# A graph network on one core: VectorE's loop over the turns of the spline passes written out with constants

## The chip, the core and the metric

The kernel runs on one core of a Trainium2 chip. The core's engines run their own instruction streams beside each other: TensorE (PE in the profile, its weight loads PEld) multiplies matrices into PSUM, VectorE (DVE) and ScalarE (ACT) work on tiles in SBUF and PSUM, GpSimd (POOL) issues here the indirect DMAs that gather rows, SyncE (SP) issues plain DMAs. They keep order among themselves by counting semaphores: one engine raises a count, another waits until it has reached a value. The metric is the time of one execution on the device in microseconds (us); lower is better.

## What is computed

A graph with 12500 nodes of 32 features and 212500 edges (source, destination, sorted by destination) goes through four parts, each closed by a residual and a layer norm: two GIN convolutions, two steps of normalised GCN propagation, three spline convolutions with batch norm, and an attention layer with four heads. The change lies in the spline convolutions. Cut to what matters:

```python
def _basis(edge_attr):
    v = edge_attr * (KS - 1)
    lo = jnp.floor(v)
    f = v - lo
    ...
    w = jnp.where(bits[None] == 1, f[:, None, :], 1.0 - f[:, None, :])
    basis = jnp.prod(w, axis=-1)
    wi = idx[..., 0] + KS * idx[..., 1] + KS * KS * idx[..., 2]
    return (basis, wi)

def _sconv(x, src, dst, basis, wi, W, R, b):
    n = x.shape[0]
    z = jnp.einsum('nc,kco->nko', x, W)
    msg = jnp.zeros((src.shape[0], W.shape[2]), x.dtype)
    for s in range(basis.shape[1]):
        msg = msg + basis[:, s, None] * z[src, wi[:, s]]
    agg = jax.ops.segment_sum(msg, dst, num_segments=n)
    cnt = jax.ops.segment_sum(jnp.ones((dst.shape[0],), x.dtype), dst, num_segments=n)
    agg = agg / jnp.clip(cnt, 1.0)[:, None]
    return agg + x @ R + b
```

## The kernel before, in words

**Passes.** The edges are handled in 1664 tiles of 128. The kernel makes a pass over them for each aggregation: gin1, gin2, gcn1, gcn2, sp1, sp2, sp3, and a last one ("collect" and "apply") for attention. In each, GpSimd gathers 128 source rows for a tile by one indirect DMA (L779), 1664 times in a spline pass (fewer in the first four, where part of the edges is handled through counts). Between two passes a node phase turns the sums into new features, and SyncE stores these as the table from which the next pass gathers.

**A spline pass.** 16 tiles are a half (104 in a pass, `HALVES`), four halves a turn (26, `TURNS`). The gathered rows go into a ring of four halves (`RING`), with one semaphore for each quarter of a slot. For half k GpSimd waits until VectorE has used the rows of half k - 4 (`u_ready`), then issues 16 gathers; it has no loop here, and its indices are in SBUF. TensorE loops over pairs of halves. VectorE runs `moments`: a prologue, then a loop of 25 turns (L1925), then the last turn written out (L1927). Both call `turn_(i, last)`.

**VectorE's turn.** For each of its four halves it makes the next half's one-hots (L1834), loads 16 places from SBUF into registers (L1894), waits for a cleared moment buffer, and then goes through 16 tiles. For each tile it adds TensorE's product to the moments at a place that a register names (`add_moments`, L1878); each addition waits for the one before it (`mom_added`) and, for each pair of tiles, for TensorE (`mom_ps`). For each pair it also makes the next right-hand sides (`one_hot_basis`, L1866), for each four tiles the next weighted rows (`weight_rows`, L1631), which wait for the gather's quarter; the next half's basis is made in four steps (L1845 to L1854), and once a half the aggregate is added (`add_aggregate`, L1886). TensorE may be up to eight tiles ahead of the additions.

**Waits.** Every `wait_ge` with a value that depends on the loop's index i gets this value from an operation of the engine's sequencer on a register (`Signal.done(phase, k)` is k plus a constant, and k is 64, 16 or 4 times i and so on). Most go through `hold` (L531), some are written in place (L1875, L1884). Where i is a Python number, the value is a constant in the instruction. TensorE's, ScalarE's and GpSimd's streams are built by functions of their own.

Of the kernel before, what the change touches and what calls it, by code (L numbers as in the profile page):

```python
# [47 lines left out]
TURNS = ET // (RING * G)  # L48
# [81 lines left out]
def build(nc, x, src_tile, dst_tile, dst_base, half_base, src_row, dst_ext, attr_tile, gW1, gb1, gW2, gb2, gW3, gb3,  # L130
          gW4, gb4, sW, sR, sb_, sg, sbe, aw, fc_w, fc_b, abias, out):
    ctx = ExitStack()
    with ctx:
# [1286 lines left out]
        def _(dve):  # L1420
# [410 lines left out]
            def moments(p):  # L1831
# [29 lines left out]
                def one_hot_basis(k, h, t):  # L1861
                    if t == 0:
                        hold(dve, "dve", close_made, k + (1 + halves * SPLINE.index(p)))
                        dve.wait_ge(basis_made.sem, basis_made.done(p, k))
                    hold(dve, "dve", mom_ps.sem, mom_ps.done(p, G * k + t + 1 - AHEAD))
                    v.tensor_tensor(vb[:, t % AHEAD:t % AHEAD + 2, :, :],  # L1866
                                    bs[:, h, t:t + 2, KS:].unsqueeze(3).broadcast_to([P, 2, K12, TW]),
                                    oh_close[:, h, t:t + 2, :].unsqueeze(2).broadcast_to([P, 2, K12, TW]),
                                    ALU.mult).then_inc(v_ready.sem, 2)
# [10 lines left out]
                def add_aggregate(k, h):  # L1880

                    first = dve.value_load(half_prev[0:1, bass.ds(k, 1)], min_val=0, max_val=N)
                    hold(dve, "dve", agg_ps.sem, agg_ps.done(p, k))
                    dve.wait_ge(agg_added.sem, agg_added.done(p, k - 1))  # L1884
                    to = acc[0:C, bass.ds(first, GW)]
                    v.tensor_tensor(to, to, ps[0:C, 4 + h, 0:GW], ALU.add).then_inc(agg_added.sem, 1)  # L1886
# [35 lines left out]
                weight_rows(p, 0, 0, 0, 1, close=True, uses=1)  # L1922
                for t in range(0, AHEAD, 2):
                    one_hot_basis(0, 0, t)
                with dve.Fori(0, TURNS - 1) as i:  # L1925
                    turn_(i, False)
                turn_(TURNS - 1, True)  # L1927
                add_aggregate(HALVES, 0)

            def places_in_half():  # L1930
# [369 lines left out]
```

## Time and profile before

| what | value |
|---|---|
| median of three plain runs | 14349.69 us (14349.25 to 14349.75) |
| profiled execution, span | 19275.3 us |
| TensorE, weight loads | 49%, 32% of the span |
| VectorE | 37% |
| ScalarE | 10% |
| GpSimd | 53% |
| mean granted TensorE clock | 0.697 of full speed |

The profile is of one execution with the hardware profiler on; on one core nothing lies around its span, which is therefore also the profiled execution's own time. It is 4926 us longer than the median of the plain runs. A row of the trace tells how an operation went in the profiled execution, and how long it took there. "Idle before" is the time that the engine had nothing running before an operation, and the name after the arrow is what the trace believes to have ended it: "issue" when nothing that it shows was waited for, "remote" when the setter of the semaphore isn't known. DVEq is VectorE's sequencer, whose register, semaphore and branch instructions are not counted as busy. A half of a spline pass begins at each L1834.

### The profile page before, as it was taken

What the parts mean: (1) busy time and instruction counts of PE and PEld (TensorE: products, weight loads), DVE (VectorE), ACT (ScalarE), POOL (GpSimd) and SP (SyncE); (2) the same over time, 40 slices, a digit from 0 to 9 for tenths busy, and PEclk for the clock granted to TensorE, in tenths of its full rate; (3) what the DMA queues carried; (4) which work ended last, traced back from release to release, by engine and by line L of the source; (5) the groups of instructions that cost most, each with busy time, mean ns of one, the idle gap of its engine ahead of it and who ended that gap; (6) DMA issues with size and microseconds to landing.
All of it is one profiled execution on the core that took longest, in us unless ns stands there. A gap on an engine that the chain in (4) does not pass through costs nothing. (4 is left out here: it accounts for less than half of the span.)

```text
span 19275.3 us, 188067 instructions
## 1 busy us (share of the span) xinstructions
PE 9537.3 (49%) x45542; PEld 6085.6 (32%) x45542; DVE 7105.4 (37%) x21441; ACT 1838.2 (10%) x1460; POOL 10279.3 (53%) x10674
## 2 busy tenths in 40 slices
PE   4444567774555554555554555554555554002224
PEld 2222222223333333433333333333344333002224
DVE  3333311112212213444444444444444444024446
ACT  3333400000000000000000000000000000000000
POOL 4555545545555554555554555554555554775551
PEclk6666667787766776777776777766777776556657
DMA  4545534444555552000000000000000001111111
GB/s 140 174 164 172 187 95 133 134 133 133 192 183 170 187 188 78 10 10 10 10 10 11 10 10 10 10 10 11 10 10 10 10 10 20 30 33 42 40 38 39
DMA packets 1034937, 1386.17 MB, mean 72 GB/s; under 512 B 318866, under 2 KB 477748, under 8 KB 1033909
## 3 DMA queue, kind: packets, MB, share of 16 engines
q10 hardware_dynamic: 550576, 1115.62, 16.5%
q0 software_dynamic: 338944, 197.81, 6.5%
q1 hardware_dynamic: 144518, 64.56, 1.5%
q14 instruction: 799, 6.55, 0.1%
q8 instruction: 100, 1.64, 0.0%
HBM read 1075.22 MB, written 302.01 MB: 71 GB/s over the span
## 5 line engine op out<-in xcount | busy, mean ns | idle before, releaser
L779 POOL DMA_INDIRECT work<-tab_sp,nodes x4992 | 4721.1, 946 | 4065.7 <-DVE work L1631 2242.7
L981 PE MATMUL ps<-work 128*128 128x192 f32 x9984 | 2766.1, 421 | 3662.8 <-DVE work L1631 2861.9
L981 PEld LDWEIGHTS ps<-work 128*128 128x128 f32 x9984 | 2051.2, 239 | 4251.7 <-DVE work L1878 2592.1
L1878 DVE TENSOR_TENSOR work<-work,ps 128x192 f32 x4992 | 1751.9, 351 | 3741.2 <-remote 1784.2
L779 POOL DMA_INDIRECT work<-tab_att,nodes x1664 | 1691.5, 1017 | 1096.2 <-issue 713.6
L779 POOL DMA_INDIRECT work<-tab_gcn,nodes x1664 | 1585.4, 953 | 1257.0 <-PE ps L875 693.6
L902 PE MATMUL ps<-nodes,work 128*96 128x384 bf16 (+1 forms) x6664 | 1976.1, 418 | 529.4 <-issue 328.8
L1709 DVE TENSOR_TENSOR big<-big,ps 32x12 f32 (+2 forms) x3936 | 619.3, 157 | 3809.0 <-remote 1487.8
L966 PE MATMUL ps<-work,wk 128*32 128x144 f32 x10080 | 1983.3, 355 | 69.2 <-issue 66.9
L779 POOL DMA_INDIRECT work<-in_x,idx x1248 | 1234.9, 990 | 1151.6 <-PE ps L875 738.0
L966 PEld LDWEIGHTS ps<-work,wk 128*32 128x32 f32 x10080 | 1250.9, 135 | 771.3 <-issue 510.7
L1298 ACT ACTIVATE work<-zero 128x2496 f32<-128x2496 f32 x318 | 725.4, 2282 | 7597.5 <-PE ps L966 3660.7
L875 PE MATMUL ps<-work 128*32 128x12 f32 (+2 forms) x7872 | 564.0, 199 | 1708.0 <-DVE big L1709 963.7
L1866 DVE TENSOR_TENSOR work<-work,ps 128x384 f32<-128x384 f32 x2496 | 1366.3, 548 | 32.6 <-issue 29.4
L779 POOL DMA_INDIRECT work<-tab_h,idx x1024 | 984.5, 961 | 737.4 <-PE ps L875 368.5
L902 PEld LDWEIGHTS ps<-nodes,work 128*96 128x96 bf16 (+1 forms) x6664 | 902.2, 142 | 1316.5 <-issue 859.2
L1003 PE MATMUL ps<-work 128*128 128x144 f32 x3584 | 557.0, 319 | 1240.5 <-issue 912.4
L875 PEld LDWEIGHTS ps<-work 128*32 128x32 f32 (+2 forms) x7872 | 479.2, 136 | 2040.6 <-DVE big L1709 1130.5
L887 PE MATMUL ps<-nodes 128*128 128x396 bf16 x2496 | 722.8, 428 | 745.4 <-ACT nodes L1256 354.4
L1256 ACT ACTIVATE nodes<-ps 128x1188 bf16<-128x1188 f32 x832 | 932.9, 1160 | 1394.9 <-remote 729.0
L1003 PEld LDWEIGHTS ps<-work 128*128 128x128 f32 x3584 | 516.7, 214 | 1281.7 <-issue 946.6
L1780 DVE TENSOR_TENSOR big<-big,ps 96x12 f32 (+2 forms) x2720 | 450.0, 165 | 1208.4 <-issue 775.2
(234 smaller groups left out, 6244.2 us busy)
## 6 DMA issues: line engine op xcount, KB each, us to landing
nodes<-counts_d ACTq DMA_DIRECT2D x468, 1056.0 KB
counts_d<-nodes ACTq DMA_DIRECT2D x104, 2376.0 KB
nodes<-counts_d ACTq DMA_DIRECT2D x144, 1320.0 KB
work<-counts_d ACTq DMA_DIRECT2D x117, 1056.0 KB
work<-tab_sp,nodes POOLq DMA_INDIRECT x4992
work<-edge_rows SPq DMA_DIRECT2D x112, 320.0 KB
edge_rows<-work ACTq DMA_DIRECT2D x104, 320.0 KB
work<-tab_gcn,nodes POOLq DMA_INDIRECT x1664
```

Source lines behind the costliest of these rows:

```text
L779: pool.indirect_dma_start(out=rows(p, r)[:, t, 0:ROW[p]], out_offset=None, in_=TABLE[p], in_offset=bass.IndirectOffsetOnAxis(ap=place, axi ...
L875: last = nc.tensor.matmul(ps[0:m, bank, q * LW:(q + 1) * LW], row(q), oh_near(p)[:, h, s * SUB + q, :], start=True, stop=True)
L887: last = nc.tensor.matmul(ps[:, 3 * (b % 2) + q, 0:w], lo_oh[:, (b // SUB) % 2, b % SUB, :], code_oh[:, b % 4, q * w:(q + 1) * w], start=T ...
L902: last = nc.tensor.matmul(to, part[:, t, 0:m], got, start=(t == 0 and m == sides[0][1]), stop=(t == NT - 1 and m == sides[0][1]))
L966: last = nc.tensor.matmul(ps[0:C, 4 + h, 0:GW], wk[:, l, kk, :], mom[:, 1 - h, kk, 0:GW], start=(kk == 0), stop=(kk == K12 - 1))
L981: last = nc.tensor.matmul(moment_place(t), u0[:, s % 2, t % SUB, :], vb[:, t % AHEAD, :, :].rearrange("p k j -> p (k j)"), start=True, sto ...
L1003: last = nc.tensor.matmul(ps[:, 4 + h, 0:GW], weighed[:, s, t % SUB, :], near_half[:, h, t, :], start=(t == 0), stop=(t == G - 1))
L1256: nc.scalar.activation(out_[:, :, :, b, :], ps[:, 3 * (b % 2):3 * (b % 2) + 3, 0:CODES // 3] .rearrange("p q (m w) -> p q m w", w=LW), ACT ...
L1298: return nc.scalar.activation(mom[:, h, :, :], zero[:, :].unsqueeze(2).broadcast_to([P, K12, GW + TW]), ACT.Copy)
L1709: v.tensor_tensor(window, window, ps[0:m, sums_bank(p, s), q * LW:(q + 1) * LW], ALU.add)\
L1866: v.tensor_tensor(vb[:, t % AHEAD:t % AHEAD + 2, :, :], bs[:, h, t:t + 2, KS:].unsqueeze(3).broadcast_to([P, 2, K12, TW]), oh_close[:, h, ...
L1878: v.tensor_tensor(to, to, got, ALU.add).then_inc(mom_added.sem, 1)
```

## The change

VectorE's loop over the first 25 turns and the separate last turn become one Python loop of 26 turns. Each turn's instructions then stand in the program once for each turn, with Python numbers in place of the register i: the values of waits, the offsets into `loc`, `all_attr`, `offs` and `half_prev`. The places that are loaded into registers are still loaded. The order of VectorE's operations and what they wait for stay as they are, and no other engine's stream is edited.

```diff
@@ -1922,9 +1922,8 @@
                 weight_rows(p, 0, 0, 0, 1, close=True, uses=1)
                 for t in range(0, AHEAD, 2):
                     one_hot_basis(0, 0, t)
-                with dve.Fori(0, TURNS - 1) as i:
-                    turn_(i, False)
-                turn_(TURNS - 1, True)
+                for i in range(TURNS):
+                    turn_(i, i == TURNS - 1)
                 add_aggregate(HALVES, 0)
 
             def places_in_half():
```

## Rows read from the trace of the kernel before

**Rows 1.** The page's head and its busy times by engine.

```profile
span 19275.3 us, 188067 instructions
PE 9537.3 (49%) x45542; PEld 6085.6 (32%) x45542; DVE 7105.4 (37%) x21441; ACT 1838.2 (10%) x1460; POOL 10279.3 (53%) x10674
```

**Rows 2.** Stretches (from:to, us): gin1, sp1, sp2, sp3; length; PE, PEld, DVE, ACT, POOL.

```profile
32.00:2389.00 2357.00, 1136.63 (x6220) 565.13 (x6217) 820.23 (x3321) 917.39 (x821) 1233.97 (x1247) 0.67 0.50 167
...
7460.00:10248.00 2788.00, 1504.92 (x6503) 1080.25 (x6504) 1299.46 (x3552) 238.02 (x116) 1572.85 (x1664) 0.73 0.07 10
10359.00:13228.00 2869.00, 1495.52 (x6500) 1078.47 (x6500) 1296.70 (x3546) 238.02 (x116) 1572.27 (x1664) 0.72 0.07 10
13339.00:16120.00 2781.00, 1514.56 (x6502) 1086.78 (x6503) 1301.91 (x3551) 238.02 (x116) 1572.52 (x1663) 0.73 0.07 10
```

**Rows 3.** The same view, sum of the eight stretches between passes and at the end.

```profile
sum 1337.30, PE 767.06 PEld 536.38 DVE 783.57 ACT 125.42 POOL 67.79; mean PE 95.88 PEld 67.05 DVE 97.95 ACT 15.68 POOL 8.47
```

**Rows 4.** Line 779: durations (ns, minimum/median/maximum), then what GpSimd waited for (us, times).

```profile
L779 POOL DMA_INDIRECT work<-tab_sp,nodes x4992: 938/944/1133, 7459.5 to 16120.2; - x200
L779 POOL DMA_INDIRECT work<-tab_gcn,nodes x1664: 938/944/4298, 4436.3 to 7333.3; - x185
L779 POOL DMA_INDIRECT work<-tab_att,nodes x1664: 938/944/2403, 16290.8 to 18907.9; - x185
L779 POOL DMA_INDIRECT work<-in_x,idx x1248: 938/944/2787, 32.2 to 2389.1; - x179
L779 POOL DMA_INDIRECT work<-tab_h,idx x1024: 938/944/9179, 2568.4 to 4268.3; - x171
...
  issue: 3396.7, 10064
  DVE work L1631: 2242.7, 291
```

**Rows 5.** Timeline of GpSimd in sp1: start, length, operation, [idle before].

```profile
9014.61 0.95 POOL L779 DMA_INDIRECT work<-tab_sp,nodes  x1 [0.31 <-issue]
9015.86 0.95 POOL L779 DMA_INDIRECT work<-tab_sp,nodes  x1 [0.30 <-issue]
```

**Rows 6.** Timeline of VectorE in sp1, then the page's group for L1878.

```profile
9014.85 0.35 DVE L1878 TENSOR_TENSOR work<-work,ps 128x192 f32 x1 [3.88 <-remote]
...
L1878 DVE TENSOR_TENSOR work<-work,ps 128x192 f32 x4992 | 1751.9, 351 | 3741.2 <-remote 1784.2
```

**Rows 7.** Timeline of VectorE: half 0 of sp2 (looped), then half 101 of sp1.

```profile
10466.94 0.36 DVE L1834 TENSOR_TENSOR ps<-iota_f,loc 128x192 f32<-128x192 f32 x1
...
10480.98 0.36 DVE L1834 TENSOR_TENSOR ps<-iota_f,loc 128x192 f32<-128x192 f32 x1
...
10262.62 0.35 DVE L1834 TENSOR_TENSOR ps<-iota_f,loc 128x192 f32<-128x192 f32 x1
...
10277.02 0.35 DVE L1834 TENSOR_TENSOR ps<-iota_f,loc 128x192 f32<-128x192 f32 x1
```

**Rows 8.** Line 1925 on VectorE's sequencer; then line 1834's idle before it (us, times).

```profile
L1925 DVEq COMPARE_BRANCH  x75: 55/63/63, 7661.3 to 16108.3; - x75
...
  issue: 178.4, 72
```

**Rows 9.** Timeline of VectorE at one of the loop's branches.

```profile
8956.78 0.68 DVE L1631 TENSOR_TENSOR work<-work,ps 128x512 f32<-128x512 f32 x1
8959.70 0.37 DVE L1834 TENSOR_TENSOR ps<-iota_f,loc 128x192 f32<-128x192 f32 x1 [2.24 <-issue]
```

**Rows 10.** Lines 1875 and 531 on VectorE's sequencer, durations in ns.

```profile
L1875 DVEq ALU_OP  x2475: 2/40/1398, 7567.9 to 16107.6; - x191
...
L531 DVEq ALU_OP  x4926: 1/40/1396, 29.0 to 19188.9; - x198
```

**Rows 11.** Instruction queue (packets, MB) in a looped turn (8957:9063), then 10235.3:10311.

```profile
q14 instruction: 6, 0.05, 0.2%
...
q14 instruction: 3, 0.02, 0.1%
```

## The prediction

> **What bounds the kernel now.** I read the page's first part, then the table of stretches, then GpSimd's gathers, and only then VectorE around the edited loop. The page says that no engine is full: GpSimd 53%, TensorE 49%, VectorE 37% [rows 1]. It also says that the profiled execution takes 19275 us, where the median of the plain runs is 14350 us. So 4926 us of what the trace shows is not in the time that I have to predict, and the first question is which waits those are.
>
> The stretches show where the profiled time lies: the first gin pass 2357 us, the three spline passes 2788, 2869 and 2781 us [rows 2]; the eight stretches between passes and at the end together 1337 us [rows 3]. In every pass GpSimd issues gathers of 128 rows, 10592 in all (4992 + 1664 + 1664 + 1248 + 1024) [rows 4]. Undisturbed, they start 1.25 us apart, 0.95 us of it busy [rows 5]. 10592 x 1.25 = 13240 us. That leaves 14350 - 13240 = 1110 us for what lies between passes, where the profile has 1337 us. The two fit with little left over: the plain run can be explained as gathers back to back in all passes, plus the stretches between. If the stretches between took all of their 1337 us in the plain run too, the spacing would be (14350 - 1337) / 10592 = 1.23 us. I take the gathers as the bound.
>
> In the profiled execution it looks different: GpSimd waits 2243 us for VectorE's L1631 (a slot of the ring that is not yet used up) [rows 4], so there VectorE's chain is the late one, at 2788 / 104 = 26.8 us for a half of 16 tiles. But look at what VectorE itself waits for: L1878 sits 3.9 us for a "remote" release, and 1784 us in all for that reason, a semaphore whose setter the trace doesn't show [rows 6]. Where these waits are absent, the same work is far quicker. A half of the second spline pass, still in the loop, takes 14.04 us from one L1834 to the next (10466.94 to 10480.98); a half of the last turn, which is already written out with constants, 14.40 us (10262.62 to 10277.02) [rows 7]. A half's gathers need 16 x 1.25 = 20.0 us. So without the waits VectorE and TensorE have 5 to 6 us of slack in each half, and GpSimd may run up to four halves ahead.
>
> **The change part by part.** It touches VectorE alone; no DMA, no other queue, no operation on data moves.
>
> The branch. The loop's COMPARE_BRANCH runs 75 times [rows 8]. After it VectorE starts nothing for 2.24 us in the example (from the end of L1631 to L1834) [rows 9]; over the three passes 72 such idles add up to 178.4 us, 2.5 us each [rows 8]. Written out, they go. For a half that is 2.5 / 4 = 0.6 us, which makes the loop's half 14.0 + 0.6 = 14.7 us against 20.0 us of gathers. Hidden: 0 us on the path. Were the cover gone, it is 178 us. The cover is the gathers' pace together with the ring.
>
> The Trainium skill ("Runtime: NRT & Kernel Launch", section on instruction fetch mechanics) says that a taken branch to code outside a small window stops the sequencer for a fetch, and that unrolling is preferred for this. The trace agrees on the idle after the branch. By that page one would book the whole idle as gain; by the gathers' spacing none. What it does here, if VectorE is the bound, is the first rival.
>
> The counted values. Each wait against a counter of the loop costs an ALU_OP of 40 ns on VectorE's sequencer: 2475 of them at L1875, and part of the 4926 at L531 (that line serves all passes) [rows 10]. Upper bound, as if all lay on the path and all of L531 belonged here: (2475 + 4926) x 0.040 = 296 us. Lower bound: the written-out half is 0.36 us longer than the looped one [rows 7], so nothing, or 75 x 4 x 0.36 = 108 us of loss. These operations run while the engine still works on the instruction before, and the addresses that come from loaded registers stay. I take 0, as the two halves are the nearest rows.
>
> The code. VectorE's turn stands 25 times more in each spline pass. One looped turn already fetches 6 instruction packets of 8 KB, most of the last turn 3 [rows 11], and no idle of the branch's kind shows in that last turn. So the fetches are not new; 0 us, hidden as above, with the branch's 2.5 us as the price of any fetch that isn't ready.
>
> The start and the end of a pass. After the last gather VectorE works off what remains, in the last turn, which was constant before. It stays as it is: 0 us.
>
> Sum: 14350 + 0 (branch, hidden) + 0 (values) + 0 (code) = 14350 us; in the profile's own time, the same edits act on a late VectorE, so 19275 should fall by 178 us and up to some 450 us although the median doesn't. The two times part company here, and the median is what is predicted.
>
> **The rivals.** First, VectorE's chain is the bound of the spline passes in the plain run too. For that the gathers must be faster than the trace shows: if the 0.30 us between two gathers is the profiler's, the spacing is 0.95 us and a half's gathers take 15.2 us; and part of VectorE's waits must be real. Then 178 us come back: 14350 - 178 = 14172 us, at the extreme 14172 - 296 = 13876 us. For it speaks that GpSimd really waits on L1631 in the profile. Against it: 10592 x 0.95 = 10062 us, plus 1337 us, leaves 2951 us that real waits must fill in just the amount that makes up the total, where the spacing of 1.25 us closes the sum without any.
>
> Second, it is the bound in some stretches alone, such as the first turns of a pass, and a third of the stalls counts: 14350 - 60 = 14290 us.
>
> Third, slower: straight code needs a new packet again and again, and if a fetch is late at two places of each turn where there was one branch, that is another 2.5 us x 75 = 187 us on VectorE: 14537 us. It decides only once a half of VectorE's work passes 20.0 us; with 14.7 + 0.6 = 15.3 us it doesn't, and it would need the first rival's conditions besides. Against it also stands the last turn without such idles.
>
> Fourth, that the edit does nothing because the values are still computed at run time: the last turn, built by the same function, has constants already, so this is put with "no change".
>
> **How the numbers follow.** Hidden behind the gathers: 0.76, within 14335 to 14365 us. VectorE bound: 0.12. Partly bound: 0.08. Slower by fetches: 0.04. The likeliest gives 14350 us. About 0.2% (29 us) is what a measurement of this kernel can tell from no change. The range reaches down to 14170 us, which takes in the partial case and half of the first rival, and up to 14370 us; what is left out is the other half of that rival, 0.04 of the slower one and a little of the likeliest. Faster by over 0.2%: 0.12 + 0.08 = 0.20; within 0.2%: 0.76; slower: 0.04.
>
> **What would show it.** In the changed profile: L1834's 178 us of idle gone (branch step); no ALU_OP at L1875 (values); no new idles marked "issue" spread over a turn (code); gathers 1.25 us apart as now; and GpSimd's wait for L1631 smaller. A median unchanged beside a shorter profiled span would confirm that the profiled waits aren't the plain run's. A median 100 us or more lower says that the spacing of 1.25 us is the profiler's own and that the first step, the bound, was read wrongly.

## The result: 22 us slower, 1.0016 of the time before

Over 20 runs each, the kernel after takes 14373.93 us (median; 14364.24 to 14382.41), the kernel before 14351.69 us (14343.21 to 14360.93). The ratio is 1.0016, 95% interval 1.001 to 1.0022. That is within the 0.2% that the prediction took as the limit of what can be told, but 20 runs do tell it from zero. The predicted 14350 us is 24 us off, and the range (14170 to 14370) ends 4 us below the median.

The first surprise is in the profile of after: its span is the plain run's time. Head, busy times, instruction queue and the chain that ended last:

```profile
span 14370.1 us, 179464 instructions
PE 8641.1 (60%) x45542; PEld 5702.3 (40%) x45542; DVE 7136.0 (50%) x21441; ACT 1825.6 (13%) x1460; POOL 10256.8 (71%) x10674
...
q14 instruction: 592, 4.85, 0.1%
...
POOL 65%; issue 22%; PE 4%; DVE 3%; DMA 3%; ACT 1%; DVEq 1%; ACTq 0%; SPq 0%; POOLq 0%
```

The edit does what it says: 8603 instructions fewer than in [rows 1], the same 21441 operations on data on VectorE, and 592 instruction packets in the whole run. And GpSimd is the bound: its gathers are 65% of the chain, "issue" (mostly the 0.30 us before each gather) another 22%.

For the comparison, the first profile of the kernel before (19275 us) is no use. The experiment before_again profiled it anew, on a chip where it took the 14351 us of the plain runs. Its head and the same parts:

```profile
span 14350.2 us, 188067 instructions
PE 8595.6 (60%) x45542; PEld 5663.4 (39%) x45542; DVE 7128.7 (50%) x21441; ACT 1827.0 (13%) x1460; POOL 10241.1 (71%) x10674
...
q14 instruction: 799, 6.55, 0.1%
```

The two spans are 19.9 us apart, close to the 22.2 us of the medians, so this pair of traces holds what is to be explained. It lies in the three spline passes. Table of stretches, from the first gather of a pass to its last (from:to, length; PE, PEld, DVE, ACT, POOL; granted clock), before_again, then after:

```profile
5506.40:7593.00 2086.60, 1410.63 (x6697) 1039.65 (x6698) 1350.12 (x3660) 244.88 (x119) 1578.86 (x1664) 0.80 0.09 14
7652.50:9733.90 2081.40, 1407.64 (x6698) 1033.23 (x6699) 1348.11 (x3659) 244.37 (x119) 1574.53 (x1664) 0.81 0.09 14
9793.30:11873.80 2080.50, 1409.34 (x6696) 1036.03 (x6696) 1349.06 (x3657) 244.87 (x119) 1573.59 (x1664) 0.80 0.09 14
sum 6248.50, PE 4227.61 PEld 3108.92 DVE 4047.28 ACT 734.12 POOL 4726.98; mean PE 1409.20 PEld 1036.31 DVE 1349.09 ACT 244.71 POOL 1575.66
```

```profile
5508.40:7599.80 2091.40, 1433.37 (x6698) 1054.95 (x6699) 1349.78 (x3660) 244.89 (x119) 1583.66 (x1664) 0.80 0.09 13
7659.50:9746.60 2087.10, 1415.83 (x6698) 1041.32 (x6699) 1352.87 (x3659) 244.56 (x119) 1580.17 (x1664) 0.81 0.09 13
9806.30:11894.80 2088.50, 1429.94 (x6697) 1053.22 (x6698) 1352.85 (x3659) 244.90 (x119) 1581.62 (x1664) 0.80 0.09 13
sum 6267.00, PE 4279.14 PEld 3149.49 DVE 4055.50 ACT 734.35 POOL 4745.45; mean PE 1426.38 PEld 1049.83 DVE 1351.83 ACT 244.78 POOL 1581.82
```

The sums differ by 18.5 us, and the last column of busy times, GpSimd's own, differs by 4745.45 - 4726.98 = 18.5 us. So the loss is not a wait: the same 4992 gathers take longer. The group of L779 says it once more, with what GpSimd waited for (before_again, then after):

```profile
L779 POOL DMA_INDIRECT work<-tab_sp,nodes x4992 | 4729.6, 947 | 1725.3 <-issue 1519.4 <-DMA tab_sp<-xc 204.1 <-DVE work L1631 1.8
```

```profile
L779 POOL DMA_INDIRECT work<-tab_sp,nodes x4992 | 4748.0, 951 | 1726.0 <-issue 1520.7 <-DMA tab_sp<-xc 204.7 <-DVE work L1631 0.6
```

A mean of 951 ns instead of 947 is 18.4 us in all. The wait for VectorE (L1631), 2243 us in [rows 4], is 1.8 and 0.6 us here. I count extra time from 0.943 us (the median is 0.944) and call a gather long from 0.953 us on: in after 374 of the 4992 are long, by 38.1 us together, against 159 by 19.4 us in before_again. In both, 2.5 us of it is one gather of 3.4 us near the start of sp1.

Which are the long ones? Timeline of GpSimd and VectorE in after (start, length, operation, [idle before]; TensorE's lines left out):

```profile
8094.05 0.55 DVE L1866 TENSOR_TENSOR work<-work,ps 128x384 f32<-128x384 f32 x1
8094.51 0.35 DVE L1845 SCALAR_TENSOR_TENSOR hat<-nodes,iota_f 128x192 f32<-128x192 f32 x1
8094.60 1.09 POOL L779 DMA_INDIRECT work<-tab_sp,nodes  x1 [0.30 <-issue]
...
8095.99 0.95 POOL L779 DMA_INDIRECT work<-tab_sp,nodes  x1 [0.30 <-issue]
...
8097.07 0.69 DVE L1631 TENSOR_TENSOR work<-work,ps 128x512 f32<-128x512 f32 x1 [0.38 <-DMA work<-tab_sp,nodes]
...
8097.24 0.95 POOL L779 DMA_INDIRECT work<-tab_sp,nodes  x1 [0.30 <-issue]
...
8098.40 0.25 DVE L1851 TENSOR_SCALAR hat<-hat 128x192 f32<-128x192 f32 x1
8098.49 0.98 POOL L779 DMA_INDIRECT work<-tab_sp,nodes  x1 [0.30 <-issue]
```

The gather at 8094.60 starts 0.09 us into L1845 and takes 1.09 us; the one at 8098.49 starts 0.09 us into the shorter L1851 and takes 0.98 us. The one at 8097.24, in the middle of L1631, takes 0.95 us. I assigned every gather of the spline passes to the VectorE operation in which it starts:

| VectorE operation at the gather's start | what it reads and writes | after: gathers, long, extra us | before_again |
|---|---|---|---|
| L1845 | nodes, iota_f (SBUF) to hat (SBUF) | 239, 194, 25.3 | 45, 31, 3.15 |
| L1849 | hat twice, to hat (SBUF) | 5, 3, 0.42 | 71, 55, 4.9 |
| L1851 | hat to hat (SBUF) | 242, 151, 7.89 | 21, 7, 0.43 |
| L1854 | hat twice, to work (SBUF) | 9, 9, 1.45 | 55, 48, 7.36 |
| L1834 | iota_f, loc (SBUF) to PSUM | 6, 2, 0.21 | 20, 8, 0.9 |
| L1866, L1878, L1631 | one operand in SBUF, one in PSUM | 3164, 5, 0.06 | 3144, 3, 0.05 |
| other operations | | 37, 5, 2.68 | 53, 4, 2.6 |
| none | | 1290, 5, 0.09 | 1583, 3, 0.05 |

(The expectations count by the operation that runs 46 ns after the gather's start; that moves some gathers that aren't long from row to row, so they have 512 and 196 gathers in the four basis steps, where this table has 495 and 192. The long ones are the same.)

The theory from this (collisions): a gather's start is held up while VectorE runs an instruction that reads two operands in SBUF, or one that reads SBUF alone and writes SBUF. The rival: the written-out code itself costs the time, and the long gathers are chance.

### The profile page after: what moved, and what is told of

It reads as the page before. It is cut to its first block, busy times and chain, and to the rows that moved or that the text cites. A ratio compares the mean times of both kernels' runs of the same rounds, so it can differ in the third digit from the quotient of the medians.

```text
span 14370.1 us, 179464 instructions
## 1 busy us (share of the span) xinstructions
PE 8641.1 (60%) x45542; PEld 5702.3 (40%) x45542; DVE 7136.0 (50%) x21441; ACT 1825.6 (13%) x1460; POOL 10256.8 (71%) x10674
## 4 chain that ended last, share of the span: by engine, by line
POOL 65%; issue 22%; PE 4%; DVE 3%; DMA 3%; ACT 1%; DVEq 1%; ACTq 0%; SPq 0%; POOLq 0%
POOL work L779 65%; DMA work<-tab_gcn,nodes 2%; PE ps L902 1%; DMA work<-in_x,idx 1%; PE ps L887 1%; PE ps L875 1%; PE ps L1086 0%; ACT nodes L1256 0%; PE ps L1003 0%; DVEq L1699 0%; PE ps L1097 0%; PE ps L1062 0%; PE ps L1114 0%; ACTq L1376 0%; DVE big L1780 0%
## 5 line engine op out<-in xcount | busy, mean ns | idle before, releaser
L779 POOL DMA_INDIRECT work<-tab_sp,nodes x4992 | 4748.0, 951 | 1726.0 <-issue 1520.7
L981 PE MATMUL ps<-work 128*128 128x192 f32 x9984 | 2660.2, 410 | 1949.0 <-DVE work L1631 1903.4
L981 PEld LDWEIGHTS ps<-work 128*128 128x128 f32 x9984 | 1983.7, 231 | 2526.3 <-issue 2233.7
L779 POOL DMA_INDIRECT work<-tab_att,nodes x1664 | 1602.7, 963 | 627.0 <-issue 627.0
L1878 DVE TENSOR_TENSOR work<-work,ps 128x192 f32 x4992 | 1740.9, 349 | 567.3 <-DVE work L1878 204.4
L779 POOL DMA_INDIRECT work<-tab_gcn,nodes x1664 | 1589.0, 955 | 553.5 <-issue 492.4
L902 PE MATMUL ps<-nodes,work 128*96 128x384 bf16 (+1 forms) x6664 | 1741.7, 383 | 165.8 <-DMA nodes<-counts_d 103.5
L966 PE MATMUL ps<-work,wk 128*32 128x144 f32 x10080 | 1752.3, 326 | 2.3 <-DVE work L1878 2.3
L1631 DVE TENSOR_TENSOR work<-work,ps 128x512 f32<-128x512 f32 x1248 | 856.8, 687 | 1537.5 <-DMA work<-tab_sp,nodes 1533.6
L779 POOL DMA_INDIRECT work<-in_x,idx x1248 | 1271.3, 1019 | 408.7 <-issue 373.7
L1866 DVE TENSOR_TENSOR work<-work,ps 128x384 f32<-128x384 f32 x2496 | 1364.4, 547 | 0.0
L966 PEld LDWEIGHTS ps<-work,wk 128*32 128x32 f32 x10080 | 1144.4, 124 | 550.5 <-issue 359.7
L779 POOL DMA_INDIRECT work<-tab_h,idx x1024 | 983.8, 961 | 332.3 <-issue 332.0
L875 PE MATMUL ps<-work 128*32 128x12 f32 (+2 forms) x7872 | 507.5, 197 | 1177.0 <-DMA work<-tab_gcn,nodes 707.0
L902 PEld LDWEIGHTS ps<-nodes,work 128*96 128x96 bf16 (+1 forms) x6664 | 836.3, 132 | 784.1 <-issue 394.8
L887 PE MATMUL ps<-nodes 128*128 128x396 bf16 x2496 | 666.0, 406 | 270.6 <-ACT nodes L1256 195.6
```

The source lines that it names most:

```text
L779: pool.indirect_dma_start(out=rows(p, r)[:, t, 0:ROW[p]], out_offset=None, in_=TABLE[p], in_offset=bass.IndirectOffsetOnAxis(ap=place, axi ...
L875: last = nc.tensor.matmul(ps[0:m, bank, q * LW:(q + 1) * LW], row(q), oh_near(p)[:, h, s * SUB + q, :], start=True, stop=True)
L887: last = nc.tensor.matmul(ps[:, 3 * (b % 2) + q, 0:w], lo_oh[:, (b // SUB) % 2, b % SUB, :], code_oh[:, b % 4, q * w:(q + 1) * w], start=T ...
L902: last = nc.tensor.matmul(to, part[:, t, 0:m], got, start=(t == 0 and m == sides[0][1]), stop=(t == NT - 1 and m == sides[0][1]))
L966: last = nc.tensor.matmul(ps[0:C, 4 + h, 0:GW], wk[:, l, kk, :], mom[:, 1 - h, kk, 0:GW], start=(kk == 0), stop=(kk == K12 - 1))
L981: last = nc.tensor.matmul(moment_place(t), u0[:, s % 2, t % SUB, :], vb[:, t % AHEAD, :, :].rearrange("p k j -> p (k j)"), start=True, sto ...
```

## The experiments

### before_again: is the long span of the first profile the profiler's?

The kernel before, unchanged.

> The kernel before, unchanged, timed against itself and profiled once more. Theory (gathers bound the spline passes; the profile of before was stretched by waits that a plain run doesn't have): a ratio of 1.000 within 0.001; if this profile is a plain one, its span is near 14350 us, its gathers start 1.25 us apart with almost no wait on L1631, and L1834 still has some 72 idles of about 2.5 us, now inside time in which VectorE would wait for gathered rows anyway. A comparison with the profile of after, stretch by stretch, should then place the 22 us: if they come from the written-out code, they lie in the three spline passes, about 7 us each; if they come from where the larger program or its data lie, they are spread over other passes too. Rival (the waits of the first profile are real in part): the span is again far above 14350 us and GpSimd waits for L1631 by more than 100 us.

Measured: 14352.05 us against 14350.72 us of before, ratio 1.0001 (0.9992 to 1.001), and a profiled span of 14350.2 us. So the profiler adds nothing. The 19275 us of the first profile are most likely a time that this kernel takes on some chips without a profiler too: in the later comparisons before took 14350 us where gathers_alone and the last written_psum ran, 14349 us beside gathers_mixed, but 19245, 20158, 19258 and 19289 us elsewhere. Both kinds are told below, apart from each other. No chip was met in two comparisons, so a property of the chip isn't told apart from its condition at that time.

### Where the kernel before takes 14350 us: written_psum

The written-out loop, in which the one-hots and the basis steps read at most one SBUF operand: copies of the iota and of `hat` lie in PSUM, and six instructions take the place of four.

```diff
-BASIS_AT = (0, 2, 4, 6)
+BASIS_AT = (0, 1, 2, 4, 5, 6)
...
-                        ins = v.scalar_tensor_tensor(flat_hat, a.unsqueeze(2).broadcast_to([P, 3 * G, KS]), 0.0,
-                                                     iota_f[:, 0:KS].unsqueeze(1).broadcast_to([P, 3 * G, KS]),
+                        ins = v.scalar_tensor_tensor(flat_p, a.unsqueeze(2).broadcast_to([P, 3 * G, KS]), 0.0,
+                                                     iota_p[:, 0:KS].unsqueeze(1).broadcast_to([P, 3 * G, KS]),
...
-                        ins = v.scalar_tensor_tensor(flat_hat, flat_hat, -1.0, flat_hat, ALU.mult, ALU.min)
+                        ins = v.tensor_scalar(flat_s, flat_p, -1.0, None, ALU.mult)
...
+                        ins = v.tensor_tensor(flat_p, flat_s, flat_p, ALU.min)
```

> The written-out loop with all basis steps and the one-hots of the spline passes reading at most one SBUF operand, in six instructions instead of four. Where the kernel before takes 14351 us: by the hold-up of gathers nearly no gather is long and the time is 14338 us (within 8), under the kernel before. If the written-out code itself costs the time, 14370 us or more. Where the kernel before takes over 19000 us: 0.997 of it, as twice before.

Measured: 14336.33 us against 14350.31 us, ratio 0.999 (0.9981 to 0.9999). It is as the collisions expect (14338 us), and outside what the rival allows (14370 us or more): the code is written out here as in after. The sum of the same three stretches (5500.8 to 7579.8, 7639.6 to 9715.9, 9777.2 to 11853.2 us), and the group of L779:

```profile
sum 6231.30, PE 4258.77 PEld 3135.69 DVE 4188.38 ACT 734.01 POOL 4709.89; mean PE 1419.59 PEld 1045.23 DVE 1396.13 ACT 244.67 POOL 1569.96
```

```profile
L779 POOL DMA_INDIRECT work<-tab_sp,nodes x4992 | 4712.5, 944 | 1726.2 <-issue 1520.9 <-DMA tab_sp<-xc 205.0 <-DVE work L1631 0.3
```

VectorE is busy 133 us longer in these stretches than in after (4188 against 4056 us), and the passes are 36 us shorter, as GpSimd's busy time is (4709.9 against 4745.5). The instructions still meet the gathers as often: 236 gathers start in L1845 and 228 in L1853 (the step from PSUM to SBUF in L1851's place), and none of these is long.

```profile
8092.87 0.35 DVE L1845 SCALAR_TENSOR_TENSOR ps<-nodes,ps 128x192 f32<-128x192 f32 x1
...
8092.95 0.94 POOL L779 DMA_INDIRECT work<-tab_sp,nodes  x1 [0.30 <-issue]
```

This gather starts 0.08 us into L1845, where that of after lost 0.15 us; it takes 0.94 us.

Three kernels on one line: the extra time of long gathers is 19.4 us (before_again), 38.1 (after), 2.5 (written_psum), and the three passes take 6248.5, 6267.0 and 6231.3 us. The first differences, +18.7 and -35.6 us, are the second ones, +18.5 and -35.7 us. So within the passes nothing is left over for the length of the code or its fetches.

### gathers_alone: the form of the instruction by itself

A small program with gathers of 128 rows back to back and a chain of equal instructions on VectorE beside them, one form for each stretch.

> Another small program in place of the kernel (its output is x, nothing of the graph network is computed): six stretches of 256 gathers from x, each of 128 rows of 32 floats, with VectorE running one form of instruction in a chain beside them: (0) nothing; (1) attr minus iota, both in SBUF, the form of L1845; (2) the same with the iota in PSUM; (3) hat with hat in place, the form of L1849; (4) hat alone, SBUF to SBUF, the form of L1851; (5) hat with hat, one of them in PSUM, written to PSUM. If gathers are held up by VectorE instructions with two SBUF operands or from SBUF to SBUF: stretches 0, 2 and 5 have gathers of 0.94 us at a spacing of 1.25 us, and 1, 3 and 4 have long ones, up to 0.94 us plus one instruction, in about the share of time in which VectorE is busy, and a mean spacing of 1.3 us or more. If no such hold-up exists, all six stretches have the spacing of the first.

Measured: the spacing that I expected did not come. In stretch 1 it is 1.251 us, in 3 1.254 us, against 1.249 us with VectorE idle; 4 of 185 and 6 of 185 gathers are long. But the forms do part, on VectorE's side. Durations (ns, minimum/median/maximum) of the five forms:

```profile
L179 DVE SCALAR_TENSOR_TENSOR hat<-all_attr,iota_f x560: 357/358/434, 334.5 to 566.1; 128x192 f32<-128x192 f32 x187
...
L179 DVE SCALAR_TENSOR_TENSOR hat<-all_attr,ps x560: 353/354/355, 656.2 to 873.4; 128x192 f32<-128x192 f32 x187
...
L183 DVE SCALAR_TENSOR_TENSOR hat<-hat x560: 357/359/432, 977.3 to 1208.6; 128x192 f32<-128x192 f32 x187
...
L183 DVE SCALAR_TENSOR_TENSOR ps<-hat,ps x560: 361/361/363, 1620.3 to 1841.6; 128x192 f32<-128x192 f32 x187
...
L196 DVE TENSOR_SCALAR hat<-hat x560: 259/260/341, 1299.3 to 1473.6; 128x192 f32<-128x192 f32 x187
```

The three forms that stay in SBUF have instructions that are 73 to 81 ns longer than their median; the two with an operand in PSUM spread by 2 ns. In stretch 1 the chain starts its instructions, for example from 401.48 us on, after 392, 391 and 467 ns, and so again and again: 1250 ns, the spacing of the gathers. It has fallen into step, so that each gather meets the border of two instructions, and there the instruction waits for the gather. So the two do exclude each other for a time. That a gather waits shows only in the few long ones: those of 1121 to 1132 ns start 45 to 51 ns after an instruction of the chain.

### gathers_mixed: out of step

The same program with one to four short instructions, in PSUM alone, between two of the form under test.

```diff
+                    for _ in range(order.randrange(1, 5)):
+                        chain(v.tensor_scalar(short, short, 1.0, None, ALU.mult))
```

> The program of gathers_alone (its output is x, nothing of the graph network is computed) with 192 gathers to a stretch, and between two instructions of the form under test one to four short ones (at random) that read and write PSUM alone, so that the gathers meet the form at all places. Seven stretches: (0) nothing; (1) attr minus iota, both in SBUF; (2) iota in PSUM; (3) hat with hat; (4) hat alone, SBUF to SBUF; (5) hat with hat, one in PSUM, to PSUM; (6) attr equal to iota, both in SBUF. If the form holds gathers up: in 1, 3, 4 and 6 nearly every gather that starts in the form's instruction with more than 85 ns of it left is longer than 0.95 us, by what is left less 81 ns; from the share of time in the form that is 40 to 45% of the gathers by 0.15 us in 1, 3 and 6 and a third of them by 0.1 us in 4, so a mean gather of 1.00 us there in place of 0.943; in 0, 2 and 5 at most 2 of 192 are long. If only the kernel's surroundings hold gathers up, all seven stretches have at most a few long ones.

Measured, for the stretches 0 to 6: the gathers' durations (ns, minimum/median/maximum).

```profile
L158 POOL DMA_INDIRECT work<-in_x,all_src x191: 941/947/1087, 13.6 to 251.4; - x191
...
L158 POOL DMA_INDIRECT work<-in_x,all_src x192: 941/947/1132, 255.5 to 496.7; - x192
...
L158 POOL DMA_INDIRECT work<-in_x,all_src x192: 941/947/962, 604.3 to 843.1; - x192
...
L158 POOL DMA_INDIRECT work<-in_x,all_src x191: 941/947/1124, 950.1 to 1190.0; - x191
...
L158 POOL DMA_INDIRECT work<-in_x,all_src x192: 941/947/1011, 1297.4 to 1536.8; - x192
...
L158 POOL DMA_INDIRECT work<-in_x,all_src x192: 940/947/957, 1612.4 to 1851.2; - x192
...
L158 POOL DMA_INDIRECT work<-in_x,all_src x192: 941/947/1093, 1970.3 to 2210.9; - x192
```

| stretch | form | long gathers of 192 | extra us |
|---|---|---|---|
| 0 | VectorE idle | 2 | |
| 1 | attr minus iota, SBUF | 23 | 2.39 |
| 2 | the same, iota in PSUM | 1 | 0.02 |
| 3 | hat with hat, SBUF | 25 | 2.37 |
| 4 | hat alone, SBUF to SBUF | 11 | 0.56 |
| 5 | hat with hat, one in PSUM | 1 | 0.01 |
| 6 | attr equal to iota, SBUF | 24 | 1.79 |

(Of stretch 0, one long gather is the program's first.) The sign is as expected: between stretch 1 and stretch 2 only the place of one operand differs, and 67 and 69 gathers start in the form. The size was not: 12% of the gathers instead of 40 to 45%, and a mean of 958 ns in place of 1000. Part of that is the filling, which took 232 ns each, so that the form ran for a third of the time; the rest is a rule that the single gathers show. In stretch 1, a gather that starts up to 45 ns after the form's instruction isn't held up; the instruction is longer instead (395 to 433 ns). One that starts 48 ns after it or later is longer by what is then left of the instruction less some 125 ns (81 ns in the expectation, which counted from 46 ns after the gather's start): at 48 ns by 189 ns, at 130 ns by 103 ns, at 228 ns by 8 ns. One example each, from the timeline:

```profile
315.96 0.36 DVE L183 SCALAR_TENSOR_TENSOR hat<-all_attr,iota_f 128x192 f32<-128x192 f32 x1
316.05 1.09 POOL L158 DMA_INDIRECT work<-in_x,all_src  x1 [0.30 <-issue]
...
317.42 0.41 DVE L183 SCALAR_TENSOR_TENSOR hat<-all_attr,iota_f 128x192 f32<-128x192 f32 x1
317.44 0.95 POOL L158 DMA_INDIRECT work<-in_x,all_src  x1 [0.30 <-issue]
```

In after the same holds: the gathers that start up to 36 ns into L1845 are not long, and the instructions beside them are (391 to 425 ns); the gather that starts 38 ns in is 188 ns longer.

The form of stretch 4, one SBUF operand to SBUF (L1851's form), has a second place at which it waits. Durations of its instruction (ns, minimum/median/maximum):

```profile
L202 DVE TENSOR_SCALAR hat<-hat x330: 259/260/510, 1298.3 to 1611.7; 128x192 f32<-128x192 f32 x165
```

If it starts 0.52 to 0.75 us after a gather's start, it ends about 1.03 us after that start, up to 250 ns late; if it starts up to 0.49 us after it, it takes its 260 ns. L1851 does the same in the kernels: in before_again the 23 that start 0.65 to 0.70 us after a gather's start take 328 to 372 ns, against a median of 251. The forms with two SBUF operands show nothing there (at most 360 ns).

The Trainium skill has this rule ("SBUF — State Buffer", section "Who interferes with whom"): VectorE and GpSimd share a pair of SBUF ports; a VectorE instruction with two SBUF inputs contends with a GpSimd instruction that reads SBUF, and one in a two-port mode, which a copy or tensor_scalar can enter, contends as well; who issues first keeps the pair and the other blocks. The traces agree on the forms and on the order deciding. They don't agree that a GpSimd instruction holds the pair for its whole length: beside a gather of 0.94 us VectorE's instruction loses at most 81 ns in gathers_alone, and at most 250 ns in gathers_mixed. Nor does stretch 6 bear out the section's inference that a tensor_tensor does not stall a GpSimd DMA: with two SBUF operands it made 24 of 192 gathers long.

### Where the kernel before takes over 19000 us

There GpSimd does wait for VectorE, and the experiments could not separate the two theories. The edits besides written_psum: looped_psum has the same operands in the loop of before; written_iota changes one operand of L1845 in the written-out loop; written_odd has `BASIS_AT = (1, 3, 5, 7)` in the written-out loop.

```diff
                         ins = v.scalar_tensor_tensor(flat_hat, a.unsqueeze(2).broadcast_to([P, 3 * G, KS]), 0.0,
-                                                     iota_f[:, 0:KS].unsqueeze(1).broadcast_to([P, 3 * G, KS]),
+                                                     iota_k.unsqueeze(1).broadcast_to([P, 3 * G, KS]),
```

First comparison (before 19244.56 us):

> The written-out kernel, with the operations that make the next half's one-hots and basis changed so that none of them reads two operands from SBUF or runs from SBUF to SBUF alone: one operand lies in PSUM; the basis takes six small steps in place of four. VectorE does slightly more work. Theory (collisions: in after 512 gathers of the spline passes begin while one of the four basis steps runs, 357 of them take longer, 35.1 us in all; in before 196, 141 and 15.8 us; the difference of 19 us is the measured one): the long gathers all but vanish, the gathers of each spline pass take about 2079 us, and the time is 14374 - 36 = 14338 us, within 8. Rival (the written-out code itself costs, by its size, its fetches or its missing register operations): the time stays at 14374 us, or rises with the added work. The fewest long gathers are expected where L1834, L1845 and their followers were.

> The same change of operands as in the run before it, made to the kernel before, with its loop. Theory (collisions): 14351 - 17 = 14334 us, within 8; what matters most: it now agrees with the written-out one within 6 us, where the two had been 22 us apart. Rival (the code itself costs): it is again about 22 us faster than the written-out one.

> The written-out kernel with a single operand changed: the first basis step (L1845) reads its iota from PSUM in place of SBUF, and nothing else. Its duration and place stay. Theory (collisions with two SBUF operands): the 194 long gathers that begin in L1845 (25.3 us) go, those that begin in L1851 (151, 7.9 us) stay: 14374 - 25 = 14349 us, within 8. Rival within the theory (any VectorE operation at that moment lengthens a gather, whatever it reads): 14374 us. Rival (the code itself costs): 14374 us.

> The written-out kernel with the four basis steps moved by one tile each (after tiles 1, 3, 5, 7 in place of 0, 2, 4, 6); the same operations with the same operands. Theory (collisions): L1845 and L1851 now begin some 265 ns later against the gathers and no longer cover a gather's start, so most long gathers go and the time falls to 14340 us, within 12; in any case the time moves from 14374 us by just the change of the summed extra length of the long gathers, within 5 us. Rival (the code itself costs): 14374 us.

Second comparison (before 20157.56 us), with the kernel after itself:

> The written-out kernel, unchanged. The four runs before this one met a chip on which the kernel before takes 19245 us, as in its first profile, where the runs of the prediction's result and of the repeat of before had 14351 us; so the long waits of that first profile are the chip's or its state's, and not the profiler's. This run tells what the edit does on the chip that it meets. On one with 14351 us for before: 14374 us again (ratio 1.0016), by collisions. On one with 19245 us, where GpSimd waits for VectorE: VectorE's chain is the late one, the 72 idles of 2.5 us before L1834 lie on it and come back, so 19245 - 178 = 19067 us, down to 18800 us with the register operations; a rival there (the waits for TensorE hide the branch too) has 19245 us.

> The written-out kernel with one-hots and basis steps that never read two operands from SBUF nor run from SBUF to SBUF alone, as in e2, whose chip was the slow one. On a chip where before takes 14351 us, theory (collisions): 14338 us, within 8, with next to no long gather; rival (the written-out code itself costs): 14374 us or more. On the slow chip: within 0.3% of before, no test of the theory.

> The same operands in the looped kernel, as in e3. On a chip where before takes 14351 us, theory (collisions): 14334 us, within 8, and within 6 us of the written-out one beside it; rival (the code itself costs): 22 us faster than the written-out one. On the slow chip it is no test of the theory.

> The written-out kernel with L1845's iota read from PSUM and nothing else changed, as in e4. On a chip where before takes 14351 us, theory (collisions of operations with two SBUF operands): the long gathers that begin in L1845 go, those in L1851 stay: 14374 - 25 = 14349 us, within 8. Rivals (any VectorE operation there collides; the code itself costs): 14374 us.

Third (before 19258.34 us) and fourth comparison (before 19288.87 us):

> The written-out loop with one operand of one instruction (the iota of L1845) read from PSUM, so that L1845 no longer reads two SBUF operands. Where the kernel before takes 14351 us: if gathers are held up by VectorE instructions with two SBUF operands, the 25 us lost under L1845 go and the time is 14349 us (within 8; VectorE's phase may shift and put other such instructions under gathers). If the written-out code itself costs the time, it stays at 14374 us. Where the kernel before takes over 19000 us, the gathers do not set the end and this says nothing on the question: 0.975 to 0.992 of before there.

> The written-out loop with all basis steps and the one-hots of the spline passes reading at most one SBUF operand, in six instructions instead of four. Where the kernel before takes 14351 us: by the collision theory nearly no gather is long and the time is 14338 us (within 8), under the kernel before. If the written-out code itself costs the time, 14370 us or more.

> The same work from PSUM in the loop of the kernel before. By the collision theory it loses its 19 us of long gathers too, and ends within 6 us of the written-out form: 14334 us (within 8). If the written-out code itself costs the time, the two forms stay 20 us or more apart, this one the faster.

> The work from PSUM in the loop of the kernel before. Where the kernel before takes 14351 us: if held-up gathers are the whole difference, it ends within 6 us of the written-out form with the same operands (14336 us). If the written-out code costs or saves anything itself, the two stay further apart: a loop at 14316 us or less would mean that the written-out code costs 20 us.

> The written-out loop with one operand of one instruction (the iota of L1845) read from PSUM. Where the kernel before takes 14351 us: if held-up gathers are the cause, the 25 us under L1845 go and the time is 14349 us (within 8). If not, 14374 us.

> The written-out loop with the four basis steps after tiles 1, 3, 5 and 7 of a half instead of 0, 2, 4 and 6: the same instructions and operands at other places. Where the kernel before takes 14351 us: if held-up gathers are the cause, the time moves with the count of gathers that start under a basis step, most likely down, to 14340 to 14360 us, and its difference from the kernel before is within 6 us of the difference of the two sums of gathers' extra time. If the place does not matter, 14374 us.

Measured, as ratios to before with their 95% intervals:

| | first | second | third | fourth |
|---|---|---|---|---|
| after | | 0.9736 (0.9705 to 0.9767) | | |
| written_iota | 0.992 (0.9894 to 0.9946) | 0.9765 (0.9738 to 0.9792) | 0.993 (0.9909 to 0.9951) | 0.9911 (0.9885 to 0.9938) |
| written_odd | 0.9884 (0.9854 to 0.9915) | | | 0.9878 (0.9854 to 0.9902) |
| written_psum | 0.9975 (0.9961 to 0.9989) | 0.978 (0.9751 to 0.981) | 0.9965 (0.9945 to 0.9985) | |
| looped_psum | 0.996 (0.9945 to 0.9976) | 1.0029 (1.001 to 1.0049) | 0.9968 (0.995 to 0.9985) | 0.9956 (0.9938 to 0.9973) |

Here the same edit makes the kernel faster: after takes 19638.98 us against 20157.56 us. The group of L779 in its profile, which answers to [rows 4]:

```profile
L779 POOL DMA_INDIRECT work<-tab_sp,nodes x4992 | 4719.8, 945 | 4226.2 <-DVE work L1631 2409.8 <-issue 1466.5 <-DMA tab_sp<-xc 349.9
```

A gather takes 945 ns, as elsewhere, but GpSimd waits 2410 us for VectorE, which itself waits for TensorE and for releases that the trace doesn't name. The chain through these two is the late one in the spline passes here, so the removed branches can count. How much they count is not settled. Written_iota gains 140 to 160 us in three comparisons, near the 178 us of the branches' idles; after gains 519 us in the second, more than all the branches and counted values of the prediction together (474 us). Written_psum and looped_psum differ by 24 us or less in the first and third, the loop being the faster, and by 498 us in the second, the written-out form being the faster. Why these chips take 19 to 20 ms, and why the second comparison is unlike the others, stays open. (The mean granted clock of before is 0.662 to 0.685 in the second, 0.694 to 0.702 in the other three.)

Three things were not measured where before takes 14350 us: looped_psum, written_iota and written_odd. So it is not shown there that the loop gains as much from the operands in PSUM, nor that L1845 alone carries 25 us.

## Why the prediction was wrong, and where it was right

**The bound: right, by a wrong reading.** Gathers 1.25 us apart do bound the kernel where it takes 14350 us; GpSimd's wait for VectorE is 0.6 us in after. But the prediction took the 4926 us between the first profile and the median for waits that a plain run doesn't have. before_again showed that the profiler adds nothing; the first profile was most likely of a chip on which the plain run is as slow. The sum that closed (10592 gathers and 1110 us between) was a good argument for the bound and none for the cause of the difference. The expected fall of the profiled span by 178 to some 450 us has the sign of what such chips show, 519 us in the plain runs of the second comparison, but there it is a plain gain.

**The branch: right.** Its idle before L1834 ([rows 8]) was 175.0 us in before_again and isn't there in after, and it cost nothing while hidden: the slack is used up by waiting for landings. What VectorE waits for before L1631 (us, times), before_again, then after:

```profile
  DMA work<-tab_sp,nodes: 1048.0, 709
```

```profile
  DMA work<-tab_sp,nodes: 1533.6, 1089
```

**The code: right.** The packets fell from 799 to 592 rather than growing, and the agreement of the extra time with the passes' lengths leaves nothing for it.

**The counted values: no time of their own, but not nothing.** The reason given, that these operations run while the engine still works on the instruction before, fails at the start of a half, where the traces show VectorE some 0.34 us earlier without them (below). [rows 7], from which 0 was taken, have the written-out half 0.36 us longer and don't show it.

**The term that failed: it wasn't in the sum.** "The gathers' pace" stood as a constant of 1.25 us, and every effect of the edit on VectorE alone was priced at 0. The pace depends on what VectorE runs at the moment a gather starts. The first trace had the sign of it in [rows 4]: a median of 944 ns and a maximum of 1133 ns for the same gather. Its price from the pair of traces is +18.7 us, of 22.2 us between the medians.

Why it rose with the edit can be read from the pair of traces. In after VectorE restarts from the landing of a quarter 1089 times of 1248, in before_again 709 times. A landing comes a fixed time after its gather's start (2.36 us, the median), so the work behind it keeps a fixed place against the next gathers, and the edit moved that place. From the restart at a half's last L1631 to the L1845 of the next half it is 2.56 us in after (the median of 279 restarts), and 2.90 us in before_again where no branch lies between (170 restarts, nine in ten of them 2.84 us or more). One of each, after and then before_again:

```profile
6447.09 0.69 DVE L1631 TENSOR_TENSOR work<-work,ps 128x512 f32<-128x512 f32 x1 [1.25 <-DMA work<-tab_sp,nodes]
...
6449.65 0.35 DVE L1845 SCALAR_TENSOR_TENSOR hat<-nodes,iota_f 128x192 f32<-128x192 f32 x1
```

```profile
6462.98 0.69 DVE L1631 TENSOR_TENSOR work<-work,ps 128x512 f32<-128x512 f32 x1 [1.35 <-DMA work<-tab_sp,nodes]
...
6465.83 0.35 DVE L1845 SCALAR_TENSOR_TENSOR hat<-nodes,iota_f 128x192 f32<-128x192 f32 x1
```

The 0.34 us are operations of VectorE's sequencer. The first addition (L1878) of a half needs the 16 places, and their load (L1894) takes 1.10 us, which outlasts the L1631 and L1834 that run beside it (0.96 us together). In before_again the load begins 0.263 us after the restart, behind two register operations that work out addresses from i, and an ALU_OP for a wait follows it; in after it begins after 0.016 us. The load in after, and the register operations of the same line in before_again:

```profile
L1894 DVEq TENSOR_LOAD <-firsts_of x312: 1093/1098/1109, 5546.7 to 11887.1; - x156
```

```profile
L1894 DVEq FUSED_REGOPS  x300: 57/57/82, 5545.0 to 11786.2; - x150
```

In the last turn of before_again, which is written out, the distance is 2.56 us as in after; behind a branch it is 5.84 us. The new place is the bad one: in after 158 of the 312 runs of L1845 start less than 100 ns before a gather, and 192 of 312 of L1851; in before_again 15 and 13. And most of the loss lies where no branch was: in the first halves of the 75 turns that before loops over (counted from L1834 to L1834), after has 100 long gathers (9.3 us extra) against 67 (7.2 us) in before_again, in the other three halves of them 255 (24.7 us) against 78 (8.6 us). So the register operations that went are the likelier cause of the shift for some 16 of the 18.7 us, the branch for the rest. This is a reading of two traces: no run had one of them taken out without the other.

**The rivals.** VectorE as the bound (14172 us) is nearer to what happens on the chips of the other kind, not on those of the median. Slower by fetches did not happen. The edit was slower by a mechanism that none of the rivals named; that the forecast came within 0.2% of the time is owed to the smallness of the effect, not to the mechanism.

**The range.** Its upper end stood 20 us above the forecast. The step that failed is the claim that an edit on a hidden engine can only cost if the cover goes; the maximum of [rows 4] gives a bound that was missing: 1133 - 944 = 189 ns, for each of 312 halves, is 59 us for one instruction of a half.

## What to carry to other kernels

An edit on an engine that is hidden can still move the bounding engine's own durations, so compare the bounding instruction's minimum, median and maximum in the trace before calling the edit free, and look at what runs beside the long ones. Where GpSimd's gathers set the pace, let VectorE's instructions beside them read one operand from PSUM: here two more instructions for each half and 133 us more work on VectorE gave a kernel that is the fastest of those measured where before takes 14350 us (0.999 of it). And when a profiled span and the median part company, profile again before reading the difference as waits that a plain run doesn't have.

## What the runs showed of the hardware

- A gather that starts about 40 ns or more (38 in after, 48 in gathers_mixed) into a VectorE instruction with two SBUF operands, or from SBUF to SBUF, is longer by what is left of it less some 125 ns, up to 189 ns; one that starts up to 36 or 45 ns into it makes the instruction up to about 80 ns longer instead.
- A tensor_scalar from SBUF to SBUF that starts 0.52 to 0.75 us after a gather's start waits too, by up to 250 ns (stretch 4: 510 against 260 ns).
- The hold-up of gathers also holds for a tensor_tensor (stretch 6: 24 of 192 gathers).
- VectorE's load of 16 places into registers takes 1.10 us (L1894), and register operations before it delay it: it began 0.263 us after a restart in the loop, 0.016 us written out.
- A chain of equal instructions falls into step with the gathers (392 + 391 + 467 ns against 1249 ns), which nearly hides the hold-up from the gathers' durations (4 long of 185).
- The same program takes 14350 us on some chips and 19245 to 20158 us on others, with nearly equal durations of a gather (945 ns for after there, 951 here), longer waits between engines (L1878 sat idle 4032 us in after there, 567 us here) and a mean granted TensorE clock of 0.695 instead of 0.771 (after on both kinds).
